# 16-bit places for TensorE's register loads, and a search moved from VectorE to GpSimd and ScalarE, in a two-layer graph network

## The reference

```python
edge_index = jnp.stack([src, dst])
h = jnp.maximum(_layernorm(x, axis=-1), 0.0)
# W = zeros((1024, 1024)).at[src, dst].add(edge_weight), then x @ W.T + bias
x = x + _L0_gnn_ref(h, edge_weight, L0_gnn_bias, edge_index)
h = jnp.maximum(_layernorm(x, axis=-1), 0.0)
# twice: mean = segment_sum(h[src], dst) / max(degree, 1); h @ W_self + mean @ W_neigh + b (relu between)
x = x + _L1_gnn_ref(h, src, dst, L1_gnn_W_self0, L1_gnn_W_neigh0, L1_gnn_b0, L1_gnn_W_self1, L1_gnn_W_neigh1, L1_gnn_b1)
return x
```

## Time and profile before

| what | us |
|---|---|
| median of 3 runs | 769.54 |
| lowest and highest run | 769.11, 769.72 |
| the profiled execution | 768.53 |
| its span, first to last instruction | 766.5 |
| TensorE busy in the span | 747.6 |
| VectorE busy in the span | 572.1 |

### The profile page before, as it was taken

How to read it: one execution, slowest core, us unless ns; L and a number is a source line. 1 busy time by engine, 2 the same in 40 slices (tenths; PEclk the granted TensorE clock), 3 DMA queues, 4 the chain that set the end, 5 groups by cost and what they waited for, 6 DMA issues and landing times.

```text
span 766.5 us, 13521 instructions
## 1 busy us (share of the span) xinstructions
PE 747.6 (98%) x4453; PEld 620.8 (81%) x4454; DVE 572.1 (75%) x819; ACT 353.5 (46%) x593; POOL 473.6 (62%) x593
## 2 busy tenths in 40 slices
PE   3999999999999999999999999999999999999998
PEld 2878888888888888888788888888888888887887
DVE  7999677877465797986779685446598857569885
ACT  7977623433353452366336745542223323245731
POOL 3000366667579999865656373436999875645992
PEclk9999999999999999999999999999999999999999
DMA  3123467665586854567683536776743868785475
GB/s 117 50 74 111 115 217 257 204 227 179 167 289 198 295 157 133 172 218 253 211 271 116 165 120 197 253 247 208 272 142 104 254 199 286 234 288 185 144 235 202
DMA packets 82984, 148.78 MB, mean 194 GB/s; under 512 B 10809, under 2 KB 21108, under 8 KB 82912
## 3 DMA queue, kind: packets, MB, share of 16 engines
q1 hardware_dynamic: 62974, 105.18, 44.0%
q10 hardware_dynamic: 19938, 42.69, 15.8%
HBM read 106.42 MB, written 41.41 MB: 193 GB/s over the span
## 4 chain that ended last, share of the span: by engine, by line
PE 97%; DVE 2%; issue 1%; DMA 0%; DVEq 0%
PE bank L1765 50%; PE bank L1819 21%; PE bank L1690 14%; PE bank L1575 4%; PE bank L1563 1%; PE bank L1596 1%; PE bank L1837 1%; PE bank L1586 1%; PE bank L1681 1%; PE bank L1592 1%; DMA dst_g<-in_dst 0%; DVE L L2004 0%; DVE R L1989 0%; PE bank L1604 0%; DVE low L1883 0%
## 5 line engine op out<-in xcount | busy, mean ns | idle before, releaser
L1765 PE MATMUL bank<-slot,split 128*128 128x512 f32 x1128 | 261.7, 390 | 0.5 <-issue 0.5
L1765 PEld LDWEIGHTS bank<-slot,split 128*128 128x128 f32 x1128 | 210.9, 188 | 44.2 <-issue 0.9
L1085 POOL TENSOR_TENSOR AT<-AT,az 128x50 int32 (+3 forms) x288 | 94.6, 329 | 115.8 <-DMA az<-asum_scratch 72.9
L1765 PE MATMUL bank<-slot,split_third 128*128 128x512 f32 x552 | 129.7, 390 | 0.0
L1765 PEld LDWEIGHTS bank<-slot,split_third 128*128 128x128 f32 x552 | 103.1, 188 | 21.4 <-issue 0.2
L1819 PE MATMUL bank<-slot,Ax 128*128 128x512 f32 (+1 forms) x510 | 119.1, 388 | 0.3
L1819 PEld LDWEIGHTS bank<-slot,Ax 128*128 128x128 f32 x510 | 93.4, 188 | 20.0 <-issue 1.4
L2149 DVE TENSOR_TENSOR slot<-T,slot 128x512 fp32r<-128x512 f32 x64 | 84.3, 1328 | 25.9 <-ACT slot L1348 22.0
L1690 PE MATMUL bank<-slot,split_m 128*128 128x512 f32 x320 | 87.9, 396 | 0.0
L1141 POOL TENSOR_TENSOR T<-T,wst 128x512 f32<-128x512 f32 x48 | 65.1, 1375 | 4.9 <-DMA wst<-in_L_gnn_W_self 4.9
L1690 PEld LDWEIGHTS bank<-slot,split_m 128*128 128x128 f32 x320 | 58.5, 188 | 11.4 <-issue 0.2
(11 more groups left out here) (234 smaller groups left out, 1196.2 us busy)
## 6 DMA issues: line engine op xcount, KB each, us to landing
stage<-hT_scratch SPq DMA_DIRECT2D x90, 256.0 KB, 3.8
wst<-in_L_gnn_W_neigh SPq DMA_DIRECT2D x56, 256.0 KB, 4.6
wst<-in_L_gnn_W_self SPq DMA_DIRECT2D x56, 256.0 KB, 3.6
x1b_scratch<-x ACTq DMA_DIRECT2D x10, 512.0 KB, 5.6
hT_scratch<-hTs ACTq DMA_DIRECT2D x10, 512.0 KB, 3.1
wst<-prod0g_scratch SPq DMA_DIRECT2D x20, 256.0 KB, 3.5
hT_scratch<-h1s ACTq DMA_DIRECT2D x20, 256.0 KB, 3.3
wst<-prod1g_scratch SPq DMA_DIRECT2D x20, 256.0 KB, 3.4
```

The costliest lines, as they stand in the source:

```text
L1085: pool.tensor_tensor(a, a, az32[:, n % NZ, pairs * pos:pairs * (pos + 1)], ALU.add) \
L1765: last = pe.matmul(dense_bank(v, which)[:, :], split_tile(v, a)[:, NT * k:NT * (k + 1)], slot[t % 2][:, b, HF * (HK * which + k):HF * (HK ...
```

## The change

Two things. First, `tab_o`, the places that TensorE loads into registers, becomes 16-bit: VectorE writes them into a tile of their own (`tab_go`, unsigned 16-bit) and the DMA moves 16 bytes a group in the place of 32. The number of loads and of values is the same; `tab_w` and `tab_a` stay 32-bit.

Second, the search for further ranges: `general`, `general_d`, `narrow` and `tab_s` are computed by GpSimd, right after its first constants. VectorE keeps `furthest` after group 2, `widest` after group 11 and the three operations on `widest` and `further` in a row after group 12. TensorE turns `furthest` in group 8 and runs `further_rows` in group 12. The conversion to integers goes to ScalarE, ahead of its copy of W in group 13, and the keys of the late groups are made by VectorE after group 36.

```diff
@@ -73,7 +73,10 @@
 NX = 4
-ROWS_AT = 10
+FURTHEST_AT = 8
+WIDEST_AT = 11
+COUNTS_AT = 13
+ROWS_AT = 12
 H0_AT = (14, 16)
...
@@ -200,7 +203,7 @@
         tab_w = sb("tab_w", [1, NG], I32, build)
-        tab_o = sb("tab_o", [1, NG * GC], I32, build)
+        tab_o = sb("tab_o", [1, NG * GC], U16, build)
         more = sb("more", [1, NG, 2], I32, build)
...
@@ -221,6 +224,7 @@
         tab_g = sb("tab_g", [NG, COLS], I32, build)
+        tab_go = sb("tab_go", [NG, GC], U16, build)
         tens = sb("tens", [NG, EP], F32R, build)
...
@@ -918,7 +922,7 @@
             sp.wait_ge(s_tab, 1)
-            sp.dma_start(tab_o[:, :], tab_g[:, OFFW:OFFW + GC]).then_inc(s_tabo, 16)
+            sp.dma_start(tab_o[:, :], tab_go[:, :]).then_inc(s_tabo, 16)
             sp.wait_ge(s_tabg, 2)
...
@@ -1052,6 +1056,18 @@
+            done = 2 + len(SHARES) + len(TIERS)
+            pool.wait_ge(s_low, 2)
+            pool.tensor_scalar(general[:, :], base_w[:, :], float(F), float(WD), ALU.is_lt, ALU.mult).then_inc(s_alone, 1)
+            pool.wait_ge(s_alone, done + 1)
+            pool.affine_select(out=general[:, :], in_=general[:, :], compare_op=ALU.is_ge, fill=0.0, base=-LATE,
+                               pattern=[[0, 1]], channel_multiplier=1).then_inc(s_alone, 1)
+            pool.wait_ge(s_alone, done + 2)
+            pool.tensor_scalar(general_d[:, :], ident[0:NG, LATE:NG], general[:, 0:1], float(TN), ALU.mult, ALU.mult) \
+                .then_inc(s_alone, 1)
+            pool.tensor_tensor(narrow[:, :], narrow[:, :], general[:, :], ALU.add).then_inc(s_alone, 1)
+            pool.wait_ge(s_alone, done + 4)
+            pool.tensor_scalar(tab_s[:, :], first[:, :], narrow[:, 0:1], None, ALU.subtract).then_inc(s_start, 1)
             pool.wait_ge(s_made, 1)
...
@@ -1307,6 +1323,13 @@
                     bases = load(act, tab_w[0:1, j:min(j + LOADS, LATE)], 0, F)
+                if j == COUNTS_AT:
+                    act.wait_ge(s_row, 1)
+                    act.wait_ge(s_later, NLATER)
+                    act.copy(more[0:1, :, :].rearrange("p b r -> p r b"),
+                             bank[7][0:1, 0:2 * NG].rearrange("p (r b) -> p r b", r=2)).then_inc(s_rng, 1)
+                    act.copy(mores[0:1, :], bank[7][0:1, 2 * NG:2 * NG + 1]).then_inc(s_rng, 1)
+                    act.copy(tier_of[:, LATE:NG], general_sums()).then_inc(s_rng, 1)
                 if j + 1 < SETS[SET_OF[j]][1]:
...
@@ -1606,6 +1629,7 @@
                 pe.wait_ge(s_spread, 1)
+                pe.wait_ge(s_alone, 2 + len(SHARES) + len(TIERS) + 3)
                 row = bank[7][0:1, :]
...
@@ -1616,6 +1640,8 @@
                 pe.wait_ge(s_h0, 1)
+                if b == 1:
+                    pe.wait_ge(s_rng, 3)
                 for k in range(KT // 2 * b, KT // 2 * (b + 1)):
...
@@ -1633,7 +1659,7 @@
                 w = SET_OF[j]
-                if j == 3:
+                if j == FURTHEST_AT:
                     pe.wait_ge(s_far, 1)
...
@@ -1930,7 +1956,7 @@
             dve.wait_ge(s_dve, shifted)
-            dve.tensor_scalar(tab_g[:, OFFW:OFFW + GC], shift[:, :], float(TW), None, ALU.mult).then_inc(s_tab, 1)
+            dve.tensor_scalar(tab_go[:, :], shift[:, :], float(TW), None, ALU.mult).then_inc(s_tab, 1)
...
@@ -2030,52 +2056,34 @@
-                if j == 0:
-                    return tick(dve.tensor_scalar(general[:, :], base_w[:, :], float(F), float(WD * TN), ALU.is_lt,
-                                                  ALU.mult))
                 if j == 2:
+                    dve.wait_ge(s_key, 2)
                     dve.tensor_reduce(furthest[:, :], key[:, :, :], AX_X, ALU.max).then_inc(s_far, 1)
                     return before
-                dve.wait_ge(s_dve, before)
-                if j == 1:
-                    return tick(dve.tensor_scalar(general_d[:, :], ident[0:NG, LATE:NG], general[:, 0:1], None, ALU.mult))
-                if j == 3:
-                    return tick(dve.tensor_reduce(general[:, :], general_d[:, :], AX_X, ALU.add))
-                if j == 4:
-                    dve.wait_ge(s_alone, 2 + len(SHARES) + len(TIERS))
-                    return tick(dve.scalar_tensor_tensor(out=narrow[:, :], in0=general[:, :], scalar=1.0 / TN,
-                                                         in1=narrow[:, :], op0=ALU.mult, op1=ALU.add))
-                if j == 5:
-                    dve.tensor_scalar(tab_s[:, :], first[:, :], narrow[:, 0:1], None, ALU.subtract).then_inc(s_start, 1)
+                if j == WIDEST_AT:
                     dve.wait_ge(s_fart, 1)
                     return tick(dve.tensor_reduce(widest[:, :], furthest_turned(), AX_X, ALU.max))
-                if j == 6:
-                    return tick(dve.scalar_tensor_tensor(out=widest[:, :], in0=narrow[:, :], scalar=float(TN),
-                                                         in1=widest[:, :], op0=ALU.mult, op1=ALU.add))
-                if j == 7:
-                    return tick(dve.tensor_scalar(further[:, :], widest[:, :], 1.0 / KA, 0.5 / KA - 0.5, ALU.mult, ALU.add))
-                dve.tensor_scalar(further[:, :], further[:, :], MAGIC, MAGIC, ALU.add, ALU.subtract).then_inc(s_spread, 1)
+                dve.wait_ge(s_dve, before)
+                if j == WIDEST_AT + 1:
+                    dve.wait_ge(s_alone, 2 + len(SHARES) + len(TIERS) + 4)
+                    before = tick(dve.scalar_tensor_tensor(out=widest[:, :], in0=narrow[:, :], scalar=float(TN),
+                                                           in1=widest[:, :], op0=ALU.mult, op1=ALU.add))
+                    dve.wait_ge(s_dve, before)
+                    before = tick(dve.tensor_scalar(further[:, :], widest[:, :], 1.0 / KA, 0.5 / KA - 0.5,
+                                                    ALU.mult, ALU.add))
+                    dve.wait_ge(s_dve, before)
+                    dve.tensor_scalar(further[:, :], further[:, :], MAGIC, MAGIC, ALU.add, ALU.subtract) \
+                        .then_inc(s_spread, 1)
                 return before
-
-            def integers():
-
-                dve.wait_ge(s_row, 1)
-                dve.wait_ge(s_later, NLATER)
-                dve.tensor_copy(more[0:1, :, :].rearrange("p b r -> p r b"),
-                                bank[7][0:1, 0:2 * NG].rearrange("p (r b) -> p r b", r=2)).then_inc(s_rng, 1)
-                dve.tensor_copy(mores[0:1, :], bank[7][0:1, 2 * NG:2 * NG + 1]).then_inc(s_rng, 1)
-                dve.tensor_copy(tier_of[:, LATE:NG], general_sums())
-                dve.tensor_tensor(key2_late[:, :, :, :], twice(key[:, LATE:NG, :], LG),
-                                  general_sums().unsqueeze(2).unsqueeze(3).to_broadcast([EP, LG, GC, 2]), ALU.add)
-
...
                 group_rows(j)
-                if j <= 8:
-                    before_it = span_of_groups(j, 0 if j == 0 else before_it)
-                if j == 14:
-                    integers()
-
+                if j in (2, WIDEST_AT, WIDEST_AT + 1):
+                    before_it = span_of_groups(j, 0 if j == 2 else before_it)
+
+            dve.wait_ge(s_rng, 3)
+            dve.tensor_tensor(key2_late[:, :, :, :], twice(key[:, LATE:NG, :], LG),
+                              tier_of[:, LATE:NG].unsqueeze(2).unsqueeze(3).to_broadcast([EP, LG, GC, 2]), ALU.add)
             h0_lo(0)
...
@@ -2086,7 +2094,6 @@
             dve.wait_ge(s_tabs, 16)
-            dve.wait_ge(s_rng, 2)
             total = count_of_further(dve)
...
```

## The result

| | before | after |
|---|---|---|
| median, us (6 runs each) | 769.33 | 817.76 |
| lowest and highest | 767.93, 770.66 | 816.34, 819.73 |
| span of the profiled execution | 766.5 | 816.1 |

The ratio is 1.0629, with an interval from 1.0611 to 1.0647. The forecast was 767.4 with a range up to 769.9: wrong in sign and far outside.

The account below looks back on a forecast made before the run. TensorE's queue was taken to pace the preparation, with VectorE the next limit: 1.68 lead - 0.1 handover + 0.64 search - 0.1 GpSimd = 2.1 us gained, so 769.54 - 2.1 = 767.4 us, range 767.0 to 767.9 (766.8 to 769.9 with rivals).

Parts of the forecast that it names:

- What bounds the kernel: Preparation: TensorE's queue sets the pace, 1.77 us a late group, with the 0.591 us register load in series; VectorE is ahead.
- Part 1: TensorE's loads of tab_o: eight 16-bit values take 0.316 us, 0.275 saved each, 9.6 us off the queue over 35 loads.
- steps of 16 bytes: TensorE's register loads: time rises about 0.26 us for each 16 bytes, so eight 16-bit values are one step, 0.316 us.
- The bounds: TensorE's 16-bit load, no row having one: from 0.316 us (0.275 saved) to 0.848 us (0.257 lost).
- Rival C: TensorE's 16-bit loads take longer: 1.5 us lost at 0.05 a load, or 8.0 us at 0.848 (777.5 us); chance 0.10.
- Rival B: TensorE's loads keep 0.59 us because registers are counted, not bytes; time 769.5 us, from 769.2 to 769.9; chance 0.25.
- What is late next: End of preparation: with shorter loads VectorE limits TensorE, whose gain is VectorE's 1.68 us lead less 0.1, plus VectorE's own gain.
- the handover: From VectorE's product to TensorE's start of a group: 0.1 us assumed (0 to 0.2), taken off the 1.68 us lead.
- the 0.1 set aside for GpSimd: Head of the kernel: GpSimd's five small operations slow VectorE's writing of the places by 0.1 us (0 to 1.0).
- Part 2: Search moved off VectorE: its product of group 36 comes 0.64 us earlier, worth nothing while TensorE leads.
- Behind the preparation: After the preparation TensorE works without a pause, tied to no other clock, so the gain is kept to the end.
- the cap on the gain: Turning of W after group 36: VectorE's copies, ending near 77.3, limit the gain to 2.6 us.

## Why the prediction was wrong, point by point

- **What bounds the kernel, right.** TensorE's queue sets the pace of the preparation and the load stands in it in series. The loads' durations grew by 49.3 us in all, and the stretch from the first of them to the turning of W by 49.1 (21.5 and 21.2 with 15 long loads). A load shorter by 0.29, with seven address computations fewer, made it VectorE's pace.
- **Part 1, the price of the 16-bit load: the step that failed.** I took 0.316 us, a saving of 0.275, and the runs have 1.93 at the median, a loss of 1.34. The rows of before had 1, 8, 9 and 16 values, and through these four points I drew steps of 16 bytes, "a width of the path that is read over". The loads of 3 and 4 values, which no row had, would have broken it. The choice rested on no row of a 16-bit load, and it carried the sign of the whole forecast.
- **The bounds, wrong too.** The upper end was "the next step up", 0.848. One value alone cost 0.316, and nothing in the rows excluded that a format off the fast path pays for each value. Eight times that is 2.5 us, a bound that would have held the 1.93.
- **Rival C had the mechanism** ("a read and an unpacking for each value") and the wrong size: 31 x 0.257 = 8.0 us, where the runs have 35 x 1.41 = 49 by the loads' means. Reading value by value is what the sizes show; whether anything is unpacked is not shown. The 0.10 that it was given was too little for an operand type without a row. Rival B, that registers are counted and nothing changes, is ruled out.
- **What is late next, right as far as it was run.** With one place for each group TensorE stands 0.06 us behind VectorE's product (0.1 was assumed), and the gain at that limit is 2.15 us for 2.1. The close match has some luck in it: the search brought 0.1 less than I took, while the handover took 0.04 less and the 0.1 set aside for GpSimd was not spent.
- **Part 2, right in the main:** nothing clear of the noise while TensorE leads (ratio 1.0004, up to 1.0021), some 0.54 us when VectorE does, for 0.64 less 0.1. GpSimd's operations end 2 us later than I had them (one `affine_select` on 40 x 1 takes 1.24 us, where three on the same shape had taken 1.04 together; why is not shown), without cost, and they don't slow VectorE's head: 0.01 us for the 0.1 that I took.
- **Behind the preparation, right:** 686.8 us for 686.6.
- **Small slips of the sum, without effect:** (1.6 + 0.6) / 35 is 0.063 and not 0.065, ScalarE's loop is 1.1 us by its own rows and not 1.2, and the cap on the gain, 79.84 - 77.3, is 2.5 and not 2.6.

## What to carry to other kernels

Fewer bytes are not fewer reads. Before a narrower type is put on a load, find a row with that type; without one, the bound on the slow side is the time of a single element multiplied by the count, not the next step of the fast path. And where a queue sets the pace, register operations count at least one for one: 38 ns more in each of eight cost a group more than a load shorter by 0.26 us brought back. Last, a median over rows of two kinds is the price of neither.

## What the runs showed of the hardware

- A register load of 32-bit values reads four at a time in about 0.26 us where they start at a multiple of four elements (4 values 0.336 us, 8 0.596, 12 0.854, 16 1.110); three values take 0.766, five 0.594, seven 1.068. By these sizes, padding three to four or seven to eight saves about 0.45 us.
- The same eight values take 0.596 us from element 0 or 4 and 1.94 from element 1 or 2. 16-bit values take 0.3 us for the first and 0.23 to 0.24 for each more on average, at 1, 2, 3, 4, 8 and 16 values from the start and at 8 from element 8. Inside the kernel's preparation the same loads scatter upwards: eight of 16 bits up to 2.35 us, with a mean of 2.03.
- Where TensorE's queue sets the pace, a longer address computation delays it by all it is longer (37 to 75 ns: chunks from 0.115 to 0.154 us), and a further operation by its duration and some 60 ns (one of 32 ns: 93 ns to the next start).
- TensorE's clock has two levels here. The 128x512 matmul that clears a bank takes 0.38 us at full rate (2.4 GHz) and 0.63 at half (1.2 GHz). Before, it is at 0.63 up to 34.3 us and at 0.38 from 37.9 on; with one place for each group and the search not moved it is at 0.38 from 24.0 on. After, it is at 0.63 for the nine in 33.7 to 77.0, at 0.38 at 82.6, at 0.63 again from 86.9 to 97.0, and at 0.38 from 99.4 on:

```profile
L1615 PE MATMUL bank<-none x9: 629/630/634, 33.7 to 77.0; 125*128 125x512 bf16 x9
```

  With the holes that the loads tear, TensorE was busy 12.44 of 16.40 us in 60.3 to 76.7, where it was busy all the time before. The profile's column of the granted clock has 0.50 for 86.9 to 93.4, but 1.00 for 60.3 to 76.7, so the first stretch shows its level in the matmuls alone. The lower rate had no part in the 48 us that can be seen: the loads' own durations fill the loss.
